# Attention beside a feed-forward net on one core: the value products of two steps issued together in every second step, with a fifth buffer of probabilities

## The reference

```python
q = xn @ Wq        # 16 heads of 16
k, v = xn @ Wk, xn @ Wv   # 8 heads of 16, each used by two query heads
scores = q k^T / 4 + where(mask, 0, -10000)
s = softmax(scores) @ v @ Wo
# mask: causal, and (nearer than 128 tokens, or the key is a landmark:
#       one of the 33% best scored tokens, widened by 2 on both sides)
h = gelu(xn @ ternary(w1)^T + b1)      # 1024 wide
g = silu(h @ ternary(w2)^T + b2)
out = x + s * g
```

## Time and profile before

| | us |
|---|---|
| runs | 701.89, 713.86, 711.15; median 711.15 |
| profiled execution, its time | 702.14 |
| its span | 700.5 |
| PE busy | 580.4 (83%) |
| ACT busy | 450.5 (64%) |
| DVE busy | 413.0 (59%) |
| POOL busy | 239.7 (34%) |
| mean granted PE clock | 0.926 |

### The profile page before, as it was taken

One profiled execution on the slowest core, in us unless ns is written; L12 is line 12 of the kernel. 1 busy time (PEld: TensorE's weight loads), 2 busy tenths in 40 slices (PEclk: granted clock), 3 DMA queues, 4 the chain that ended last, 5 costly groups with the idle time before them and its releaser, 6 DMA issues. The chain is left out here.

```text
span 700.5 us, 11117 instructions
## 1 busy us (share of the span) xinstructions
PE 580.4 (83%) x3764; PEld 300.0 (43%) x3764; DVE 413.0 (59%) x1041; ACT 450.5 (64%) x568; POOL 239.7 (34%) x284
## 2 busy tenths in 40 slices
PE   0436818999899989999899879999899899799973
PEld 0424602564344535544353626544353545324512
DVE  4939974876839547867656539858465654510111
ACT  1302417788777765797678655787578667797770
POOL 2020023334243533333543324431543353335431
PEclk9858977999999979999999969999999989899995
DMA  7000422211313233302132252203032223022101
GB/s 225 0 5 7 103 62 87 66 33 34 83 44 98 55 103 82 89 23 64 46 95 56 64 146 68 62 9 96 20 98 56 61 83 95 27 72 65 49 15 47
DMA packets 51092, 45.43 MB, mean 65 GB/s; under 512 B 9041, under 2 KB 45394, under 8 KB 51026
## 3 DMA queue, kind: packets, MB, share of 16 engines
q1 hardware_dynamic: 48898, 42.77, 22.4%
q10 hardware_dynamic: 2128, 1.84, 0.9%
HBM read 11.28 MB, written 4.19 MB: 22 GB/s over the span
## 5 line engine op out<-in xcount | busy, mean ns | idle before, releaser
L1551 ACT ACTIVATE f_probs<-sc_ps,shift 128x1024 f32<-128x1024 f32 (+3 forms) x384 | 333.3, 902 | 106.8 <-PE sc_ps L1460 101.6
L1460 PE MATMUL sc_ps<-f_q_stack,f_k_stack 104*128 104x512 bf16 (+3 forms) x768 | 197.8, 348 | 34.8 <-ACT f_probs L1551 17.6
L1477 PE MATMUL att_ps<-f_probs,f_v_sb 128*32 128x512 f32 (+3 forms) x1536 | 168.7, 513 | 9.9 <-POOL f_probs L1599 9.8
L1592 POOL TENSOR_SCALAR_AFFINE_SELECT f_probs<-f_probs 128x512 f32<-128x512 f32 x128 | 93.4, 730 | 130.6 <-ACT f_probs L1551 130.4
L1460 PEld LDWEIGHTS sc_ps<-f_q_stack,f_k_stack 104*128 104x128 bf16 x768 | 48.6, 100 | 200.5 <-ACT f_probs L1551 119.8
L1599 POOL TENSOR_TENSOR f_probs<-f_probs,f_near 128x512 f32<-128x512 f32 x64 | 75.5, 1180 | 107.2 <-ACT f_probs L1551 107.2
L1585 POOL TENSOR_TENSOR f_h_lo<-f_hid,f_h_hi 128x512 fp32r<-128x512 f32 x32 | 42.4, 1324 | 94.7 <-DVE f_h_hi L1642 94.7
L1403 PE MATMUL aux_ps<-w2T,f_h_hi 128*128 128x256 f32 x256 | 71.9, 315 | 0.3
L1477 PEld LDWEIGHTS att_ps<-f_probs,f_v_sb 128*32 128x32 f32 x1536 | 31.4, 109 | 73.7 <-issue 45.6
L1403 PE MATMUL aux_ps<-w2T,f_h_lo 128*128 128x256 f32 x256 | 62.8, 279 | 0.0
L1512 ACT ACTIVATE f_hid<-aux_ps,b_sb 128x512 f32<-128x512 f32 x64 | 43.2, 690 | 23.7 <-PE aux_ps L1393 15.8
(11 more groups left out here) (150 smaller groups left out, 738.9 us busy)
## 6 DMA issues: line engine op xcount, KB each, us to landing
f_q_stack<-f_q_parts SPq DMA_DIRECT2D x192, 64.0 KB
f_k_stack<-f_k_parts SPq DMA_DIRECT2D x96, 64.0 KB
xn<-in_L_attn_hidden_states SPq DMA_DIRECT2D x4, 1024.0 KB, 6.5
f_attT<-f_att_raw SPq DMA_DIRECT2D x128, 32.0 KB
f_rden_bc<-f_den SPq DMA_DIRECT2D x64, 64.0 KB
s_w_nat<-in_L_ffn_w SPq DMA_DIRECT2D x2, 1024.0 KB, 8.1
out_y<-xn SPq DMA_DIRECT2D x4, 512.0 KB, 3.2
xn<-in_L_attn_hidden_states SPq DMA_DIRECT2D x3, 512.0 KB, 4.0
```

The lines of the kernel that those rows point to most:

```text
L1460: last = pe.matmul(sc_ps[:, 2 * u + hh, lo:CH], k_stack[0:KROWS + T, h // REP, kb * P:(kb + 1) * P], q_stack[0:KROWS + T, SLOT[n], 2 * u + ...
L1477: last = pe.matmul(att_ps[32 * q:32 * q + 32, n % 2, lo:CH], v_sb[:, kb, j * VW:j * VW + 32], probs[:, i % NPROB, q, lo:CH], start=(kb == ...
L1551: act.activation(probs[:, i % NPROB, us, lo:CH], sc_ps[:, us, lo:CH], ACT.Exp, bias=shift[:, 0:1], scale=HD ** -0.5).then_inc(exp_done, 1)
L1592: pool.affine_select(out=block_probs, in_=block_probs, compare_op=ALU.is_ge, fill=0.0, base=0, pattern=[[0, NQ], [1, P]], channel_multipli ...
```

## The change

`values` is no longer called in each step from 3 on. In every even step i from 4 on, PE issues `values(i - 4)` and `values(i - 3)` one behind the other, between `scores(i, 0)` and `scores(i, 1)`; in odd steps it issues only the two halves of scores. So the values of even steps come one step later, and those of odd steps (the group ends among them) where they came before. `probs` gets a fifth buffer (8 KB more in each partition), and NPROB, by which ACT's wait and all buffer indices go, becomes 5. No instruction is added or taken away.

```diff
@@ -1126,7 +1126,7 @@
-                probs = tile("probs", [P, 4, NQ, CH])
+                probs = tile("probs", [P, 5, NQ, CH])
@@ -1186,7 +1186,7 @@
-                NPROB, BEHIND = 4, 3
+                NPROB, BEHIND = 5, 3
@@ -1484,7 +1484,8 @@
                                     if i < NSTEP:
                                         scores(i, 0)
-                                    if i >= BEHIND:
+                                    if i % 2 == 0 and i >= BEHIND + 1:
+                                        values(i - BEHIND - 1)
                                         values(i - BEHIND)
                                     if i < NSTEP:
                                         scores(i, 1)
```

## The result

The changed kernel takes 718.67 us (median of four runs, 715.52 to 722.13), the kernel before 709.69 in the four runs that stand against them; the ratio is 1.0167, 95% interval 1.0109 to 1.0226. Ratios and intervals here leave out single runs that lie over 1.5% above the fastest run of their kernel (here the 713.86 of before), so a ratio is not that of the medians. The change makes the kernel slower, by 1.7% as the best estimate, under the 2% that the prediction held likeliest; the interval reaches 2.3%. On the profiled execution of 702.14 us the ratio makes 713.9 us; the 712 forecast are a ratio of 1.0141, inside the interval. The two profiled executions stand further apart: span 716.4 against 700.5 us, +15.9, where +9.9 was forecast. In later rounds the kernel before had medians of 703.88 to 705.87 us; the changed kernel was not timed in them.

A forecast was written before the change was run, and what follows sets the result against it. PE was taken to bound steps with jobs, PE and ACT to be nearly equal and take turns in steps without. 702.1 + 4.0 (last turn) + 5.9 (three turns that prepare) gave 712 us, range 695 to 730.

The forecast's parts named there:

- The sum: Whole kernel: 702.1 + 4.0 (last turn) + 5.9 (three turns that prepare) = 712 us.
- The loop: Pair e, second half of scores of e to that of e+2, without jobs: ACT idles during two values; pair 42 +0.69.
- The saving: Fewer changes of product shape on PE: 0.19 us per PE-bound pair, 18 us if PE bounded all.
- The faster rival: PE bounds nearly all pairs (e even, o = e+1), so the saved shape changes stay: 684 us, chance 0.11.
- pairs 14 and 16 in the turns that prepare: Around the ffn_up ahead of step 16: pair 14 costs 0.3 us, pair 16 costs 0.2.
- Half absorbed: In turns that prepare, PE's waits for POOL and DVE take up 1.7 us of +3.6, leaving +1.9 each.
- The start of the last turn: First pair of steps 0 to 15 costs 0.5 us by the same loop.
- The fifth buffer is needed: Probs in the new order: otherwise exponentials of even step e wait for values(e-4); by itself worth nothing in the old order.
- The clock rival: New gaps in stalled pairs halve PE's clock in a third of them: 741 us, chance 0.07.

The follow-up runs named there:

- short exponentials: Each exponential takes only the first 128 columns of each head, in both orders: order of before 703.38 us, changed order with five buffers 697.31 us.
- A: Kernel before with five buffers and two values together only beside ffn_down (odd steps 7 to 13, 35 to 41): 702.82 us, ratio 0.997 to before.
- D: As A, but with odd step 35 left in place: 702.67 us, ratio 0.993 to the kernel before.
- B: Changed kernel, but no two values together in odd steps 3, 7 to 13 and 35 to 41: 721.74 us.
- C: Changed kernel with DVE's near-mask products on 16 of 128 columns: 713.4 us; the same masks in the order of before: 702.16 us.

## Why the prediction was right, point by point

- **The sum.** The direction was right, and so was a loss under 2%. By the ratio the kernel loses 1.7%, forecast 1.4%. By the two profiles it loses 15.9 us for 9.9: the turns that prepare 10.3 for 5.9, the last 4.7 for 4.0, and 1.0 ahead of the first scores, where nothing was forecast. (Three times the prediction's +1.9 are 5.7, not 5.9; 712 stays.)
- **The loop.** Right in mechanism and, where it was written out, in size. Pairs 42 and 44 of the last turn: forecast 5.21 and 4.78, measured 5.20 and 4.79; its pairs 24, 26 and 28: forecast 4.14, 5.50 and 5.19, measured 4.14, 5.50 and 5.18. Pairs 18 to 24 of the second turn: forecast +2.0 (0.6, 0.5, 0.7, 0.2), measured +2.17; pair 44 there was forecast at +0.85 and cost only 0.38. Pairs 18 to 44 of the last turn: forecast +4.6, measured +5.0. That this came so close is in part luck: pair 18 takes 5.64 us in this profile and 7.4 to 7.6 in the four others with the same loop (last section). The short exponentials show for pairs 42 and 44 that ACT's 1.0 us is what closes it.
- **The saving.** Forecast 0.19 us for each pair bounded by PE, measured 0.25 with short exponentials and 0.15 to 0.26 in the real `ffn_down` pairs. A little too small. The Trainium skill's page "TensorEngine Tiling (Array Packing)", section Key Properties, says that a change of tiling mode drains the engine; the pairs that PE bounds agree with it, without showing that the drain is the cause. What the trace adds is where it holds: in the changed kernel only seven or eight of the 24 pairs of a turn keep the saving.
- **The faster rival** was told off by its own condition, that PE have over 1 us of other work behind the second half of e. In kernels A and D, which take only such pairs, the saving stands in all of them but 34 (in A +0.32 in the turns that prepare, where the prediction had +0.4 for the changed kernel, and -0.06 in the last).
- **The mis-sized term: pairs 14 and 16 in the turns that prepare.** The prediction gave 0.3 and 0.2 us, measured are +1.32 and +0.28 (the same in all three turns), so 3.3 us more than forecast in all, from the profiles. It let PE's own queue decide there, and saw the values of step 12 only as moved. In fact the moved values cost 0.83 us (the kernel that leaves them), since two values now stand between the halves of step 16. And what PE gained in steps 6 to 13 (0.8 to 1.2 us) is lost again, all of it against B, 0.5 to 0.6 of it in A and D: DVE comes to the split of the hidden values without a gap and holds `ffn_up` at 11.0 us, while with room on DVE it takes 9.95. The last turn, in which DVE prepares nothing, behaves as forecast: pair 14 +0.26, pair 16 -0.55; but pair 16 there varies by 0.65 between two profiles of the order of before, so its figure may be chance.
- **Half absorbed.** Of 10.5 us of waits for POOL and DVE the prediction let 5.1 take up loss. They shrank by 3.6 and 1.6, in sum 5.2. That the loss ran into them one by one isn't shown, since the stretch of steps 26 to 33 varies by 1 to 4 us between profiles (+4.0 us there in one turn of kernel A, which leaves these steps alone). The agreement of the sums may be chance.
- **The start of the last turn** (first scores to the second half of step 6): forecast +0.5 for the first pair, profile +1.8; how much of it is the clock isn't settled, but kernel D and the fifth buffer alone, which leave steps 0 to 5 as they were, have +0.9 and +1.25.
- **The end**, which the prediction left out, came 1.1 us shorter behind the second half of step 46: four values in a row don't wait 0.79 us for a mask as before, and the last `out_proj` took 5.13 us for 5.90. The latter isn't the change's: the granted clock was 0.62 from 706 to 712 us, against 0.54 from 690 to 696 before.
- **"The fifth buffer is needed"**: wrong in size, 0.3 us in two pairs of a turn; for the whole the two kernels' intervals overlap.
- **The clock rival** didn't come by the stalls in the changed kernel; with four buffers it came in one stalled pair; below.

## What to carry over

Where two engines hand two halves of a buffer back and forth, write the loop out, from one hand-over back to itself, in start-to-start times: it gave pairs 42 and 44 of the last turn to 0.01 us, while the busy share (83%) said that the matrix engine was the bound. Batch work of one kind only where the engine has other work behind it that covers the partner's turn. And what one engine gains counts only up to the next place that another one paces: look which engine runs without a gap there, for a gain ahead of it is handed back.

## What the chip showed besides

**Short gaps cost no clock but once; behind waits of 2.4 to 4 us it often fell.** In the stalled pairs 42 and 44 of the changed kernel, with gaps of 0.29 to 0.88 us one behind the other, the granted clock stays at 1.00 (stretches: busy us by engine, PEclk, DMA share, GB/s):

```profile
684.00:688.00 4.00, 3.60 (x24) 0.84 (x22) 0.00 (x0) 2.92 (x4) 1.16 (x1) 1.00 0.14 33
688.00:692.00 4.00, 2.83 (x23) 0.77 (x23) 0.00 (x0) 3.00 (x4) 3.09 (x4) 1.00 0.00 0
```

The Trainium skill's page "TensorE: Matmul & The Clock Gate", section "A second HAM failure mode: psum-queue depth-cycling", tells of a kernel in which frequent small idle times make the clock swing. Of the five profiles with this loop and full exponentials four don't show that in the stalled pairs of steps 18 to 24 and 42 to 46, but for pair 18 behind the long wait ahead of step 17. The fifth, with four buffers, does once, in pair 42 of the second turn: PE and the stretches there, behind gaps of 0.48, 0.40 and 0.40 us:

```profile
386.77 0.95 PE L1460 MATMUL sc_ps<-f_q_stack,f_k_stack 104*128 104x512 bf16 x2 [0.40 <-ACT f_probs L1552]
387.65 3.22 PE L1477 MATMUL att_ps<-f_probs,f_v_sb 128*32 128x512 f32 x16
```

```profile
386.00:388.00 2.00, 1.60 (x8) 0.32 (x10) 1.93 (x8) 1.72 (x2) 0.20 (x1) 0.72 0.10 22
388.00:390.00 2.00, 2.00 (x12) 0.40 (x8) 0.95 (x2) 0.35 (x1) 0.95 (x1) 0.50 0.21 50
```

So what the clock rival said did happen, but once: in one pair of one profile, which took 7.12 us where it takes 5.49 in the other turns of the same profile, far from a third of the pairs. Ahead of step 17 of the last turn PE waits 3.16 to 4.05 us in the kernels with full exponentials, and in each of these profiles the clock is at 0.50, 1.2 GHz, at that wait or soon behind it, as in the earlier trace rows; how many steps fall into it differs. With short exponentials and the changed order the wait is 2.52 us, and the clock stays at 1.00. It also fell in the third turn around a wait of 2.38 us for POOL ahead of step 32 (changed kernel) and behind one of 2.74 (before), which is one reason why steps 26 to 33 vary. In the changed kernel:

```profile
619.16 2.04 PE L1460 MATMUL sc_ps<-f_q_stack,f_k_stack 104*128 104x512 bf16 x4 [3.17 <-ACT f_probs L1552]
```

```profile
620.00:622.00 2.00, 1.74 (x5) 0.26 (x4) 0.00 (x0) 1.81 (x3) 0.00 (x0) 0.50 0.00 0
622.00:624.00 2.00, 2.00 (x19) 0.73 (x18) 0.00 (x0) 1.53 (x2) 0.00 (x0) 0.50 0.00 0
624.00:626.00 2.00, 1.56 (x4) 0.30 (x3) 0.69 (x1) 1.05 (x2) 0.00 (x0) 0.69 0.03 5
```

In kernel C the wait, 3.18 us, ends at 612.62, and the clock goes to 0.50 only near 614 and stays there through the stalled pair 18:

```profile
614.00:616.00 2.00, 1.77 (x8) 0.33 (x10) 0.00 (x0) 1.82 (x3) 0.00 (x0) 0.50 0.00 0
618.00:620.00 2.00, 1.65 (x5) 0.15 (x3) 0.00 (x0) 1.89 (x2) 0.00 (x0) 0.50 0.14 31
620.00:622.00 2.00, 2.00 (x7) 0.33 (x10) 0.00 (x0) 1.88 (x3) 0.46 (x1) 0.50 0.17 39
```

That pair then takes 7.5 us where it took 5.6 in the changed kernel. In four of the five profiles with this stalled pair (four buffers, step 12 in place, B, C) it takes 7.4 to 7.6 us; the changed kernel's own is the exception. A stalled loop that begins at half clock is dearer than one at full clock. Why the clock falls now earlier and now later isn't settled by these runs.
